# Gated attention of a fused two-layer decoder: the engines' rounds in another order, gate buffers 8 to 12

## What is computed

```python
q = silu(x @ Wq); k = silu(x @ Wk); v = x @ Wv            # 16 heads of 64
cum = cumsum(-softplus(x @ Wa + ba), axis=1)
attn = (q @ k.T) * exp(cum_i - cum_j)   # where j <= i, else 0
o = attn @ v
o = (o - mean(o)) / sqrt(var(o) + EPS)  # over all rows and the 64 columns of a head
o = o * gn_w + gn_b
return (o * sigmoid(x @ Wg)) @ Wo
```

## Time and profile before

| what | value |
|---|---|
| time, median of 3 runs | 1566.49 us (1565.9 to 1568.96) |
| the profiled execution's own time | 1570.07 us |
| its span in the trace | 1568.3 us |
| PE busy | 1279.3 us (82%) |
| DVE busy | 829.3 us (53%) |
| ACT busy | 835.9 us (53%) |
| POOL busy | 493.3 us (31%) |

### The profile page before, as it was taken

The page is one execution under the profiler, slowest core; times in us unless marked ns, Lnnn a source line. Parts: engine busy times, 40 slices in busy tenths (PEclk is TensorE's granted clock), DMA queues, the critical chain, the costliest instruction groups (busy, mean ns, idle before and its releaser), DMA issues.

```text
span 1568.3 us, 22559 instructions
## 1 busy us (share of the span) xinstructions
PE 1279.3 (82%) x6903; PEld 738.9 (47%) x6934; DVE 829.3 (53%) x2634; ACT 835.9 (53%) x1893; POOL 493.3 (31%) x463
## 2 busy tenths in 40 slices
PE   5999999999999997987644967788888896796462
PEld 2434443443344335544424955566666664454251
DVE  3543453354444426467642337777676876557425
ACT  4777677677767734544312635565565653353121
POOL 2555455545545522221433531101011111122232
PEclk9999999999999999998776989999999998898677
DMA  7234322220000000000024841000000000000053
GB/s 212 56 73 87 60 56 55 55 78 1 1 1 1 1 1 0 1 1 1 14 94 135 247 136 41 1 2 1 1 1 1 1 1 28 1 1 7 26 150 94
DMA packets 77701, 67.56 MB, mean 43 GB/s; under 512 B 5040, under 2 KB 68656, under 8 KB 77328
## 3 DMA queue, kind: packets, MB, share of 16 engines
q1 hardware_dynamic: 73488, 57.69, 15.0%
q0 software_dynamic: 3520, 7.27, 1.3%
q10 hardware_dynamic: 576, 1.16, 0.2%
HBM read 37.69 MB, written 28.41 MB: 42 GB/s over the span
## 4 chain that ended last, share of the span: by engine, by line
PE 64%; DVE 17%; issue 8%; ACT 7%; SPq 2%; POOL 2%; DMA 1%; another core or an unknown queue 0%; ACTq 0%; POOLq 0%; DVEq 0%
PE bank L554 8%; PE bank L536 7%; PE bank L544 7%; PE bank L483 6%; PE bank L659 3%; PE bank L526 3%; PE bank L616 3%; PE bank L630 3%; PE bank L724 3%; PE bank L732 2%; PE bank L862 2%; PE bank L830 2%; PE bank L645 2%; DVE work L1396 2%; ACT work L1002 1%
## 5 line engine op out<-in xcount | busy, mean ns | idle before, releaser
L1935 POOL TENSOR_TENSOR work<-work 128x512 f32<-128x512 f32 x256 | 266.5, 1041 | 271.4 <-DVE work L1404 271.4
L1002 ACT ACTIVATE work<-bank,work 128x512 f32<-128x512 f32 x256 | 176.6, 690 | 116.6 <-DVE work L1396 116.6
L1396 DVE TENSOR_REDUCE work<-bank 128x1 f32<-128x512 f32 x256 | 176.6, 690 | 77.7 <-PE bank L536 77.3
L544 PEld LDWEIGHTS bank<-cst,work 128*128 128x128 f32 x1024 | 110.5, 140 | 163.8 <-issue 105.1
L544 PE MATMUL bank<-cst,work 128*128 128x128 f32 x1024 | 159.7, 283 | 6.3 <-ACT work L1010 6.1
L1404 DVE RECIPROCAL work<-work 128x1 f32<-128x1 f32 x256 | 41.9, 164 | 223.3 <-ACT work L1002 223.0
L1010 ACT ACTIVATE work<-bank 128x512 f32<-128x512 f32 x256 | 152.8, 597 | 0.5 <-PE bank L544 0.5
L536 PE MATMUL bank<-work 64*128 64x512 f32 x512 | 144.5, 641 | 3.4 <-ACT work L1002 3.4
L2013 POOL TENSOR_TENSOR work<-work 128x512 f32<-128x512 f32 x32 | 41.0, 1283 | 323.0 <-PE bank L862 287.0
L554 PE MATMUL bank<-work 128*64 128x512 f32 x512 | 137.4, 617 | 0.7 <-ACT work L1010 0.7
L1975 POOL TENSOR_TENSOR work<-work 128x1232 f32<-128x1232 f32 (+1 forms) x32 | 55.5, 1735 | 253.1 <-DVE work L1477 253.0
(11 more groups left out here) (241 smaller groups left out, 2429.8 us busy)
## 6 DMA issues: line engine op xcount, KB each, us to landing
xs<-gat SPq DMA_DIRECT2D x18, 1040.0 KB, 11.5
W<-in_w SPq DMA_DIRECT2D x30, 322.0 KB
W<-in_w SPq DMA_DIRECT2D x23, 193.0 KB
work<-xs SPq DMA_DIRECT2D x62, 65.0 KB
gat<-yt SPq DMA_DIRECT2D x12, 256.0 KB, 3.2
work<-in_w SPq DMA_DIRECT2D x9, 322.0 KB
W<-in_v SPq DMA_DIRECT2D x1, 2048.0 KB, 11.5
x_ext<-in_x SPq DMA_DIRECT2D x4, 256.0 KB, 8.7
```

What stands on the lines that cost most here:

```text
L544: m = nc.tensor.transpose(out[:, k * P:(k + 1) * P], pA[u % 5][:, k * P:(k + 1) * P], ident)
L1002: A(pA[u % 5], bank[u % 3][:, :], ACT.Exp, bias=nmax[:, u % 8:u % 8 + 1], accum_out=rsum[0][:, u % 8:u % 8 + 1]).then_inc(sem("a_e"), 1)
L1396: V.tensor_reduce(nmax[:, u % 8:u % 8 + 1], bank[u % 3][:, :], AX, ALU.max, negate=True)\
L1935: G.tensor_tensor(pA[u % 5], pA[u % 5], rsum[1][:, u % 8:u % 8 + 1].to_broadcast([P, S]), ALU.mult)\
```

## The change

On PE, `d_decays` and the first `d_decay_to` move between the q and the k projection; value products come one at a time at three places of a round (after the scores: `V_MID`; after the k transpose: `V_LATE`; after the output: `V_END`); `d_alpha` moves behind the scores and `d_sums` ahead of `d_out`. On ACT, `d_decays` is cut into `d_el` and two `d_exps`, which stand around the k tanh; `d_affine` of four tiles becomes two of two, tiles 0 and 1 at the end of s = 0 or 4 and tiles 2 and 3 in the next round ahead of `d_o`; `d_softplus` moves forward. On DVE, the q half of `d_silu` goes ahead of `d_st`; `d_z` goes forward; the closing steps move to rounds 0, 1, 2, 6, 7, 8, 10, 11 and 13 (before: 0 to 2, 4 to 6, 8 to 10) and, with `d_gated`, stand ahead of `d_stats` and no longer behind it; `d_split_x` moves from s = 5 to s = 4 or 3. `turn_x` for batches 1, 2, 3 is at rounds 3, 9, 14 (before: 3, 7, 11) and ahead of the tail of the batch before. The gate's tanh gets four more buffers, `thE`, in the memory of `gat`, for pairs 12 to 15 and 24 to 27. The set of instructions is the same; their order, waits and buffers differ.

```diff
--- before
+++ after
@@ -125,6 +125,7 @@
         gat = sb("gat", [P, 16 * XW])
         xb = gat[:, 0:NT * D]
+        thE = [gat[:, i * S:(i + 1) * S] for i in range(4)]
         oh = sb("oh", [P, NB * NT * 2 * E])
@@ -239,6 +240,18 @@
         ALPHA_AT = (4, 2, 2)
         SUMS_AT = (5, 4, 4)
+        CLOSE_AT = {0: (1, 0), 1: (1, 1), 2: (1, 2), 6: (2, 0), 7: (2, 1), 8: (2, 2), 10: (3, 0), 11: (3, 1), 13: (3, 2)}
+        TURN_AT = {3: 1, 9: 2, 14: 3}
+        V_MID = {3: (0, 1, 1), 4: (0, 1, 3), 6: (1, 0, 1), 7: (1, 0, 2)}
+        V_LATE = {2: (0, 1, 0), 3: (0, 1, 2), 7: (1, 0, 3)}
+        V_END = {5: (1, 0, 0)}
+        def th_buf(g):
+            if g < 12:
+                return thD[g % 8]
+            return (thE, thD[4:8], thD[0:4], thE, thD[4:8])[(g - 12) // 4][g % 4]
         wqE, wkE, wvE, woE = (W0[:, i * 512:(i + 1) * 512] for i in range(4))
@@ -885,47 +898,50 @@
                 d_decay_to(0, 0)
                 d_decay_to(0, 1)
+                def value(at, g):
+                    if g < 32 and g % 8 in at:
+                        nb, hf, t = at[g % 8]
+                        if g // 8 + nb < NB:
+                            d_v(g // 8 + nb, hf, t)
                 for g in range(32 + 4):
                     b, s = g // 8, g % 8
+                    more = g < 32 and b + 1 < NB
                     if 1 <= g <= 32:
...
                         d_proj(g + 1, 0)
-                        d_proj(g + 1, 1)
                         d_decays(g + 1)
                         d_decay_to(g + 1, 0)
+                        d_proj(g + 1, 1)
                     if g < 32:
                         d_scores(g)
+                    value(V_MID, g)
+                    if more and s == ALPHA_AT[b]:
+                        d_alpha(b + 1)
                     if g + 1 < 32:
...
                         d_kturn(g)
+                    value(V_LATE, g)
+                    if more and s == SUMS_AT[b]:
+                        d_sums(b + 1)
                     if 2 <= g < 34:
                         d_out(g - 2)
+                    value(V_END, g)
                     if s in (2, 6) and g >= 6:
...
                         tail(PD + b - 2, s + 8)
-                    if g in (3, 7, 11):
-                        turn_x(PC + g // 4 + 1)
-                    if g < 32:
-                        if b:
-                            tail(PD + b - 1, s)
-                        if s in (2, 3):
-                            d_v(b, 1, 2 * s - 4)
-                            d_v(b, 1, 2 * s - 3)
-                        if b + 1 < NB:
-                            if s == ALPHA_AT[b]:
-                                d_alpha(b + 1)
-                            if s == SUMS_AT[b]:
-                                d_sums(b + 1)
-                            if s in (6, 7):
-                                d_v(b + 1, 0, 2 * s - 12)
-                                d_v(b + 1, 0, 2 * s - 11)
+                    if g in TURN_AT:
+                        turn_x(PC + TURN_AT[g])
+                    if b and g < 32:
+                        tail(PD + b - 1, s)
@@ -1195,25 +1211,27 @@
                 A(v3(vD[hf], NT)[:, t, :], where["d_v", n][:, :], ACT.Copy).then_inc(sem("d_vs"), 1)
-            def d_decays(g):
-                b, p = g // 8, g % 8
+            def d_el(g):
                 act.wait_ge(sem("d_lp"), g + 1)
...
                 A(elD[g % 3], bank[0][:, :], ACT.Exp, scale=-1.0).then_inc(sem("d_el"), 1)
-                if p == 0:
-                    act.wait_ge(sem("d_lcs"), b + 1)
-                if g >= 2:
-                    act.wait_ge(sem("d_at"), 2 * (g - 1))
-                for hh in range(2):
-                    act.wait_ge(sem("d_la"), 2 * g + hh + 1)
-                    for c in range(NT):
-                        k = c * H + 2 * p + hh
-                        i = A(dmD[g % 2][:, (NT * hh + c) * P:(NT * hh + c + 1) * P], bank[1 - hh][:, c * P:(c + 1) * P],
-                              ACT.Exp, scale=-1.0, bias=lcD[b % 2][:, k:k + 1])
-                    i.then_inc(sem("d_dm"), 1)
+            def d_exps(g, hh):
+                b, p = g // 8, g % 8
+                if hh == 0:
+                    if p == 0:
+                        act.wait_ge(sem("d_lcs"), b + 1)
+                    if g >= 2:
+                        act.wait_ge(sem("d_at"), 2 * (g - 1))
+                act.wait_ge(sem("d_la"), 2 * g + hh + 1)
+                for c in range(NT):
+                    k = c * H + 2 * p + hh
+                    i = A(dmD[g % 2][:, (NT * hh + c) * P:(NT * hh + c + 1) * P], bank[1 - hh][:, c * P:(c + 1) * P],
+                          ACT.Exp, scale=-1.0, bias=lcD[b % 2][:, k:k + 1])
+                i.then_inc(sem("d_dm"), 1)
@@ -1224,9 +1242,13 @@
                 else:
                     act.wait_ge(sem("d_gp_"), g + 1)
-                    if g >= 8:
+                    if 8 <= g < 12:
                         act.wait_ge(sem("d_og"), g - 7)
-                    A(thD[g % 8], src, ACT.Tanh, scale=0.5).then_inc(sem("d_th"), 1)
+                    elif g >= 16:
+                        act.wait_ge(sem("d_og"), g - 11)
+                    elif g == 12:
+                        act.wait_ge(sem("M_cb"), NB)
+                    A(th_buf(g), src, ACT.Tanh, scale=0.5).then_inc(sem("d_th"), 1)
@@ -1237,12 +1259,12 @@
                 A(o_slot(PD + g // 8, g % 8), bank[5][:, :], ACT.Copy).then_inc(sem("d_o"), 1)
-            def d_affine(k):
+            def d_affine(k, pairs):
...
                 b, p0 = k // 2, 4 * (k % 2)
-                for i in range(4):
+                for i in pairs:
                     o = o_slot(PD + b, p0 + i)
@@ -1256,38 +1278,49 @@
                 d_tanh(0, 0)
                 d_tanh(0, 1)
-                d_decays(0)
+                d_el(0)
+                d_exps(0, 0)
+                d_exps(0, 1)
+                def value(at, g):
+                    if g < 32 and g % 8 in at:
+                        nb, hf, t = at[g % 8]
+                        if g // 8 + nb < NB:
+                            d_v(g // 8 + nb, hf, t)
                 for g in range(32 + 4):
                     b, s = g // 8, g % 8
+                    more = g < 32 and b + 1 < NB
                     if g + 1 < 32:
                         d_tanh(g + 1, 0)
+                        d_el(g + 1)
+                        d_exps(g + 1, 0)
                         d_tanh(g + 1, 1)
-                        d_decays(g + 1)
+                    value(V_MID, g)
+                    if g + 1 < 32:
+                        d_exps(g + 1, 1)
                     if 1 <= g <= 32:
                         d_tanh(g - 1, 2)
+                    if more and s == ALPHA_AT[b]:
+                        d_softplus(b + 1)
+                    if s in (1, 5) and g >= 8:
+                        d_affine((g - 8) // 4, (2, 3))
+                    value(V_LATE, g)
                     if 2 <= g < 34:
                         d_o(g - 2)
+                    value(V_END, g)
                     if s in (0, 4) and g >= 8:
-                        d_affine((g - 8) // 4)
+                        d_affine((g - 8) // 4, (0, 1))
                     if g >= 16:
                         tail(PD + b - 2, s + 8)
-                    if g in (3, 7, 11):
-                        keep_xT(PC + g // 4 + 1)
-                    if g < 32:
-                        if b:
-                            tail(PD + b - 1, s)
-                        if s in (2, 3):
-                            d_v(b, 1, 2 * s - 4)
-                            d_v(b, 1, 2 * s - 3)
-                        if b + 1 < NB:
-                            if s == ALPHA_AT[b]:
-                                d_softplus(b + 1)
-                            if s == SUMS_AT[b]:
-                                d_kdec(b + 1)
-                            if s in (6, 7):
-                                d_v(b + 1, 0, 2 * s - 12)
-                                d_v(b + 1, 0, 2 * s - 11)
-                d_affine(7)
+                    if g in TURN_AT:
+                        keep_xT(PC + TURN_AT[g])
+                    if b and g < 32:
+                        tail(PD + b - 1, s)
+                    if more and s == SUMS_AT[b]:
+                        d_kdec(b + 1)
+                d_affine(7, (0, 1, 2, 3))
@@ -1842,7 +1875,7 @@
                     dve.wait_ge(sem("d_on"), 4 * k + i + 1)
                     o = o_slot(PD + b, p0 + i)
-                    V.scalar_tensor_tensor(out=o, in0=thD[p0 + i], scalar=1.0, in1=o, op0=ALU.add, op1=ALU.mult)\
+                    V.scalar_tensor_tensor(out=o, in0=th_buf(4 * k + i), scalar=1.0, in1=o, op0=ALU.add, op1=ALU.mult)\
                         .then_inc(sem("d_og"), 1)
@@ -1860,40 +1893,41 @@
                 for g in range(32 + 4):
                     b, s = g // 8, g % 8
+                    more = g < 32 and b + 1 < NB
+                    if g + 1 < 32:
+                        d_silu(g + 1, 0)
```

(30 more changed lines are left out.)

## The result

The changed kernel is slower: median 1579.8 us (1576.1 to 1583.2) against 1568.9 us of the kernel before on the same chips, a ratio of 1.0074 (95% interval 1.0054 to 1.0094), some 11 us. The prediction said 1560.4 us, 0.4% faster. The profiled execution has a span of 1578.2 us, 9.9 us over that of before.

A forecast was written before the change was run, and what follows sets the result against it. PE was taken as nearly full, with only 49.4 us of idle time to win. Batches counted zero and rounds 0 to 14 6.1 us won: 1566.49 - 6.1 = 1560.4 us (1564.0 for the profiled execution), range 1543 to 1571.

The forecast's parts named there:

- The loop: Output to statistics, copy, tanh, silu, gate projection: 1.8 us to spare; whatever is put in beyond that stops PE.
- Part 1: Value products spread: second-product waits of 2 to 3 us a batch go, new waits at gate projection and k's silu; zero.
- Part 2: Affines, el, gate buffers: 3.1 us removed; d_gated (2.67 us) ahead of d_stats makes statistics 3.4 us late: 3.0 added.
- Part 5: DMAs and queues: SP's transfers neither move nor wait differently, POOL's product is ready a round early; nothing.
- Part 3: Work queued behind the copy on ACT, and sums ahead of the output: projections wait about 2.2, 1.9 and 2.1 us.
- the sum: All terms together: both batches taken as zero, leaving 6.1 us won in rounds 0 to 14.
- The full walk: Hand timing of a batch, three waits charged in full: 91.8 us against 89.8, the last 83.3 against 83.4.
- three waits: Waits of 2.2, 2.1 and 1.9 us a batch that the hand timing charges in full; the forecast took zero instead.
- Part 4: Closings at other rounds: gains and losses by round in rounds 1 to 14 sum to 6.2 us won, taken as 6.1.
- Part 6: Clock in round 5: low behind 3.87 us idle, put at 3 to 4 us; would stay up behind shorter new pieces.
- The loop late: Rival: statistics over 1.8 us late behind d_gated and closings, clock falls in round 5; 1571, at worst 1575; chance 0.17.
- the prediction's signs: Right if ACT's L1845 waits go, DVE bounds rounds 7 and 11, pair 14's d_state comes about 6 us earlier, among others.

The follow-up runs named there:

- experiment 9: Kernel 7 with the value products in twos at the round's end again: 0.9941 of the kernel before, 3 us below kernel 7, intervals overlapping.
- 8: The kernel before with the four gate buffers and the value products spread: 1.0039 of the kernel before, 11 us slower than with the buffers alone.
- Experiment 3: The changed kernel with GpSimd's product started behind the statistics, not at the output's end: 1.0003 of the kernel before, 11 us below the changed kernel.
- experiment 2: The changed kernel with the closings back in rounds 0 to 2, 4 to 6, 8 to 10, still ahead of the statistics: 1.0079 of the kernel before.
- 14: The changed kernel with only the closing of batch 3 moved, to rounds 9, 10 and 13: 1.0099 of the kernel before.
- experiment 17: The changed kernel with only the decay sums back at the end of PE's round: 1.0025 of the kernel before, 7.7 us off the changed kernel.
- experiment 5: The changed kernel with d_gated alone back behind the statistics, closings still ahead: 0.9974 of the kernel before.
- 7: The changed kernel with d_gated and closings behind the statistics and batch 3's closing in rounds 9, 10 and 13: 0.9962 of the kernel before.
- 15: The changed kernel with d_gated and closings behind the statistics and the closings in their old rounds: 0.9923 of the kernel before.
- 16: The changed kernel with d_gated and closings behind the statistics, closings in old rounds, decay sums at the end of PE's round: 0.9875 of the kernel before.

## Why the prediction was wrong

*What bounds it.* The loop (output, statistics, copy, tanh, silu) was the right object: every experiment that moved the time moved something into it or out of it.

*Part 1, value products.* Net zero held in the new order (experiment 9). The 1.9 us of waiting at the gate projection in step 0 was 1.18 us. The bank of q, which part 1 names, is what costs 11 us in the old order (8).

*Part 2, affines and gate buffers.* The waits went as predicted, and the buffers are worth 4.9 us alone. The first failing step is `d_gated` "2.67 us": that duration was read where a product lies beside it for 0.3 us only. Ahead of the statistics it is 3.57 us. Part 5 looked at the product only for when it is ready and called the queues nothing; what it does to VectorE's operations was in no term. "3.1 us removed, 3.0 added" a group was too kind: putting `d_gated` back wins 15.7 us over seven groups, 2.2 a group. Experiment 3, which removes the standing beside the product (`d_gated`'s and the closing sums'), wins 11.

*Part 3 and the sum.* The full walk had 91.8 and 83.3 us for the two batches, so 1.9 us lost together: 2.0 in the first and a tenth won in the last, not "2.0 us lost a batch". 92.7 and 84.7 were measured, 4.2 us lost. The forecast took zero, on the ground that the walk charged three waits "to the last tenth", and so left out the right sign. Kept, it would have given 1562.3 us, still a gain. Where the clock stayed full, as the walk had assumed, the last batch took 83.1 us (2 and 14): the walk, 83.3, was right there in sum, which is luck in part, since its `d_gated` was too short; 1.6 of the 84.7 us are the clock's.

*Part 4, the closings.* Rounds 1 to 6 were right in sum (6.6 us predicted, 5.5 measured, and block D began 2.1 us sooner). In rounds 6 to 14 the terms sum to 0.4 us lost; 13.3 were. From one `d_at` to the next, round 9 gained 2.4 us (2.6 predicted), round 11 lost 3.3 (2.8) and round 13 lost 1.2 (2.2), but rounds 10 and 12, predicted to gain 1.3 together, lost 2.9 and 3.6. In both the clock is at its lower level in the changed kernel (columns as above, the granted clock is the third number from the end):

```profile
1065.00:1070.00 5.00, 5.00 (x20) 4.15 (x21) 2.26 (x6) 2.22 (x7) 0.00 (x0) 0.57 0.00 0
1090.00:1095.00 5.00, 4.42 (x20) 2.98 (x19) 4.42 (x13) 2.23 (x7) 0.00 (x0) 0.50 0.00 0
```

where it was full before. In round 10 the k projection had waited 2.17 us for the copy of x, and the scores after it took 2.08 us for 1.16; in round 12 it had waited 2.34 us for `d_var`:

```profile
1061.86 0.47 PE L832 MATMUL bank<-W_low 128*128 128x512 f32 x1 [2.17 <-ACT xT_all L981]
...
1062.84 2.08 PE L843 MATMUL bank<-work 64*128 64x128 f32 x16
...
1088.57 0.47 PE L832 MATMUL bank<-W_low 128*128 128x512 f32 x1 [2.34 <-DVE work L1857]
```

Beside the clock there are the closing sum and round 9's `d_gated` next to GpSimd's product (1.0 and 0.9 us) and the sums ahead of the output in round 12. No run splits the rest among them.

*Part 6, the clock.* This is the second failing step: the walk had the full clock throughout, and no term of the sum paid for less. Part 6 looked at round 5 alone. By the Trainium skill, "TensorE: Matmul & The Clock Gate", section "Why this matters for your kernels", long idle gaps between bursts of matmuls bring the clock down and short ones do not. The trace doesn't agree, if pieces shorter than the 3.87 us of the earlier trace rows are short, as part 6 took them to be: the kernel before itself had the clock low in round 5 behind 2.24 us. Nor does a longer wait always bring it down: in round 10 of the same kernel TensorE waited 3.02 us and the clock stayed full.

```profile
1009.24 0.45 PE L808 MATMUL bank<-work,sel 128*128 128x512 bf16 x1 [2.24 <-ACT work L1204]
...
1009.40:1012.90 3.50, 3.50 (x14) 2.93 (x13) 1.94 (x5) 2.50 (x9) 0.00 (x0) 0.51 0.01 2
...
1069.30 0.47 PE L819 MATMUL bank<-W_low 128*128 128x512 f32 x1 [3.02 <-DVE work L1755]
```

In round 21 it stayed full behind 1.92 us in the changed kernel and fell behind the same 1.92 us in experiment 2.

What one low piece costs, round 26 shows. From round 23 on the changed kernel and experiments 2, 14 and 17 are the same program. Rounds 23 to 25 take 28.5 us in all four and rounds 27 to 30 take 43.4; in round 26 each waits 2.57 us for the copy of x. Only the clock differs. Experiment 2, the changed kernel and experiment 17, round 26:

```profile
1254.94:1266.16 11.22, 8.49 (x69) 6.29 (x69) 8.53 (x17) 5.81 (x15) 1.31 (x1) 1.00 0.01 2
1251.53:1264.35 12.82, 10.25 (x71) 7.33 (x69) 8.72 (x17) 5.80 (x15) 1.31 (x1) 0.87 0.01 2
1246.50:1260.61 14.11, 11.38 (x69) 8.28 (x69) 8.72 (x17) 5.91 (x15) 1.30 (x1) 0.76 0.01 2
```

So 3.4 us at the lower level cost 1.6 us and 6.9 us cost 2.9. In block D, up to its last `d_state`, the changed kernel was at the lower level for 30.7 us in seven pieces, the kernel before for 10.3 us in two, both in rounds 5 and 6. At the price of round 26 that is an estimate of 13 to 14 us of the 16 by which the profiled execution missed the forecast of 1564.0, whose walk had none; 7 to 8 of the 13.3 us in rounds 7 to 14, where the kernel before had the clock full (0.92 for 1.00); and 3 of the 4.2 us of the batches. The lower clock isn't a cause apart from the order: in rounds 18 and 26 the clock falls in the changed kernel behind 2.57 us of waiting, and with the product moved (3), behind 1.5 us, it stays full. How much of the 11 us of experiment 3 goes through the clock isn't shown. Nor is the clock all: between 1060 and 1120 us it was 0.91 in experiment 5, 1.00 in 7 and 0.94 in 15, and rounds 7 to 14 took 100.8, 97.0 and 92.3 us, so the clock isn't what orders them.

*The decay sums* were seen in part 3, 0.9 us and a wait of 2.1 us that was taken to be there before as well. Part 4 had them behind `d_kd` and `d_sp`, 0.95 us, and 1.55 us long. Measured they cost 7.7 us in the change (with them at the end of the round, round 5 falls from 16.8 to 10.4 us and rounds 7 to 14 by 4.4 together; the two batches rise by 2.8, the clock being low in rounds 18, 22 and 26 for longer). From `d_at` to `d_at` round 5 was put at 14.4 us and took 16.8, with the clock low for 6.8 us of it; the gain that it could have had was not seen.

*The rivals.* The loop late was the right rival and named the right place, with a chance of 0.17 and 1571 us. Its size was short, since it had neither VectorE's standing beside the product nor the clock of rounds 10 to 26; its 3.5 us for the clock were for round 5 alone. Of the prediction's signs, DVE did bound rounds 7 and 11 (13.0 and 13.8 us), ACT's wait for `d_gated` went, and the k projection waited for the copy of x; but `d_state` of pair 14 came 7.9 us later, counted from `d_state(0)`, and not 6 earlier.

*Left open:* what decides whether the clock falls behind a wait of about 2 us, and so how much of each experiment's gain goes through it; why the old and the new rounds of the closings are equal while they stand ahead of the statistics, apart from the clock in 2 and 14. Keeping `d_gated` ahead with its product elsewhere and the sums behind, at once, wasn't tried.

## What to carry to other kernels

Before moving an operation on VectorE, look at what GpSimd does at the new place: the duration in the old trace holds only for the old neighbours. This was seen here for operations with both inputs in SBUF and for one small `tensor_scalar`, and not for the statistics, which read PSUM. In a hand-ordered pipeline find the loop that crosses the engines, and count what is put into it ahead of the step that others wait for; seven groups of four tiles cost 16 us more ahead of the statistics than behind them. Where a walk with the trace's durations gives a sign, don't round it to zero; where it opens new waits of 2 us on TensorE, let the sum have a term for the lower clock. And undo parts of a many-part change one by one: here the parts that 16 keeps, 1.25% together, hid behind three bad ones.

## What the runs showed that was not expected

- VectorE's operation on two SBUF inputs stands still for most of a GpSimd elementwise operation that runs beside it: 1.77 us for 0.68, and 2.18 for 1.14 for four small ones. A `tensor_scalar` of 128x4 took 0.99 us for 0.24. Once it was GpSimd that stood, 3.41 us for 1.28. The statistics, which read PSUM, took 0.70 us beside a product in the kernel before.
- One changed wait on GpSimd moved the whole kernel by 11 us down or 10 us up, depending on VectorE's order.
- TensorE's clock fell to 1.2 GHz behind single waits of 1.92 to 2.57 us, and stayed full behind one of 3.02 us. The same program with the same wait of 2.57 us kept the full clock in one execution, and had it low for 3.4 us in another and for 6.9 us in a third.
